# A graph network kernel: 28 blocks of plain-node rows made in round 3 instead of round 2

## The chip, the core and the metric

The program runs on one core of a Trainium2 chip. The metric is the device time of one execution in microseconds. Each engine (PE for matrix products, DVE and ACT for vector and scalar work, POOL, SP for issuing transfers) has its own instruction stream and waits for the others by semaphores.

## The reference, cut to what matters

Four graph layers follow each other, each added to its input and normalised. The second is a graph convolution that runs four rounds on 100,000 nodes of 64 numbers with 50,000 edges. Cut to it:

```python
def _L1_gnn_ref(x, edge_index, W, b, gamma, beta, num_rounds):
    loops = jnp.arange(n)
    src = jnp.concatenate([edge_index[0], loops])
    dst = jnp.concatenate([edge_index[1], loops])
    deg = segment_sum(ones, dst); dis = rsqrt(deg); norm = dis[src] * dis[dst]
    for _ in range(num_rounds):                     # 4 rounds
        h = x @ W
        agg = segment_sum(h[src] * norm[:, None], dst) + b
        x = layernorm(agg) * gamma + beta
    return x
x = _layernorm(x + _L1_gnn_ref(x, edge_index, ..., 4), axis=-1)
```

A node with no incoming edge has only its own loop: its row in a round is a product with W and a normalisation of its own row of the round before, with no gather. Here such rows are called plain. The kernel makes this plain form for every node, and the rows of nodes that are targets of edges are made in addition from gathered sums.

## The kernel before, in words

The convolution is done by `round_pass`, called as r1a and r1b (round 1 in two parts, which also make plain rows one round further), r2, r3 and r4, with a small `fix_pass` after a round that mends the rows in which a run of edges crosses partitions. Rounds don't overlap: `fix_pass` starts after SP and all engines are done with the round.

A pass goes over chunks of T = 14 columns of 128 edges each; there are 28 chunks (`CHUNKS`), two per step. For each chunk POOL issues 14 indirect gathers of 128 rows (line 2602), into four buffers of 7. DVE makes running sums along the edges, 7 columns at a time (`half`, line 2702, tile r_acc), adds the target's own row (`finish`, line 2735, tile r_gx), and the result is the input of the unit of targets.

A unit is a block of 128 x 14 rows, 128x896 numbers, that goes through: turned by PE (line 2851, tile r_ps_t), copied by ACT (2930, r_gt), multiplied by PE (2876, 2879 and 2882), squared by ACT (2936), summed over the features by DVE (2758), then root, reciprocal and a product with the result, tile r_y or, for targets, r_yt (2787 in round 2, 2789 in the others), and stored by SP. Each chunk has, besides its unit of targets, `nn` units of plain nodes and `ns` units of source rows (the nodes from which edges start, one row per edge), which SP loads (r_in). Units of one chunk come in the order plain, source, target. Before the change round 2 has nn = 2, ns = 1: four units per chunk. Round 3 has nn = 0, ns = 1: two.

In round 3 the source unit is also joined: its result for the whole layer is made at once. PE makes two products for it (dense1g into r_ps_v, gw into r_ps_g), DVE makes r_v (2774, 2776), adds the layer's input (r_r, 2779, loaded as r_x), sums again (2795) and writes r_y with one more number per row (2813, 2814). Round 3 also clears a table with SP's stores of r_blank. Round 2 keeps an extra copy of the product in SBUF by ACT (r_vs, 2939), so that the PSUM buffer is free early; round 3 doesn't.

The order on each engine is written out by `staged`: at each unit's slot an engine does one part for this unit, another for the unit some slots before. In slots behind the unit: PE turns 1 and multiplies 2 slots later, ACT squares 2 later, DVE sums and scales 3 later, the join ends 5 later, and SP stores 4 later (6 with a join). DVE's order within a slot is: sum of the product, sum of the join, running sums of this slot, end of the join, end of the unit. Every chunk's first half of running sums is done in the slot of the unit before the targets, its second half and r_gx in the targets' slot. Results go through two buffers of r_y (`y_free` waits until the one of two units ago is stored).

Of the kernel before, what the change touches and what calls it, by code (L numbers as in the profile page):

```python
# [9 lines left out]
D = 64  # L10
# [2236 lines left out]
def staged(eng, steps, units, most):  # L2247


    back = -(-most // units)  # L2250

    def run(body):
        def turn(i):
            for u in range(units):
                def ago(n):
                    at = i + (u - n) // units if (u - n) // units else i
                    out = isinstance(at, int) and not 0 <= at < steps
                    return () if out else ((at, (u - n) % units),)
                body(ago)
        for i in range(back + 1):  # L2260
            turn(i)
        if steps > back + 1:
            with eng.Fori(back + 1, steps) as i:
                turn(i)
        for i in range(steps, steps + back):
            turn(i)
    return run


CHUNKS = TILES // T  # L2270
# [136 lines left out]
                                             rest[:, 2, :].unsqueeze(1).to_broadcast([3, T, D])))  # L2407


def round_pass(nc, t, name, first_chunk, chunks, tkind, table, own, nkind, by_node, by_source, t_out, clear=None):  # L2410

# [1 line left out]
    nps = nn + ns  # L2415
    steps, units = chunks // 2, 2 * (nps + 1)
    first, tjoin, njoin = tkind == "first", tkind == "join", nkind == "join"
# [8 lines left out]
    with ExitStack() as ctx:  # L2426
        def sb(n, shape, dt=F32):
            return ctx.enter_context(nc.sbuf_tensor(f"{name}_{n}", shape, dt))
# [4 lines left out]
        def sems(n, count=2):  # L2433
            return [sem(f"{n}{u}") for u in range(count)]
# [19 lines left out]
        yt = sb("yt", [P, 2, T, D + 1 if tjoin else D])  # L2454
        y = sb("y", [P, 2, T, YW])
# [19 lines left out]
        in0_ok, y_stored = sems("in0_ok", units), sems("y_stored", units)  # L2475
# [16 lines left out]
        def is_t(u):  # L2492
            return u % (nps + 1) == nps

        def sub(u):
            return u // (nps + 1)

        def of_source(u):
            return nn <= u % (nps + 1) < nps

        def joined(u):
            return tjoin if is_t(u) else njoin

        def order(i, u):
            return i * (units // 2) + u // 2
# [7 lines left out]
        def after(eng, stage, i, u):  # L2513

            if valid(i):
                eng.wait_ge(stage[u % 2], order(i, u) + 1)
# [13 lines left out]
        def n_back(i, u, n):  # L2530

            for _ in range(n):
                i, u = back_to(i, u, 1, lambda w: not is_t(w))
            return i, u
# [2 lines left out]
            return bass.ds((first_chunk + i * 2 + s) * T, T)  # L2537

        def n_chunk(i, u):
            return (i * 2 + sub(u)) * nn + u % (nps + 1)  # L2540

        def s_columns(i, u):
            return bass.ds(((i * 2 + sub(u)) * ns + u % (nps + 1) - nn) * T, T)
# [1 line left out]
        def n_index(u):  # L2545
            return sub(u) * nps + u % (nps + 1)

        def slot(u):
            return n_index(u) % 2

        def j_slot(u):
            return u % 2 if tjoin else n_index(u) % 2

        def n_slot(u):
            return n_index(u) % IN
# [1 line left out]
        def nodes(tab, i, u):  # L2557
            features = X1 if tab is t.nodes1 else slice(0, D)
            return tab[0:NP, :].rearrange("(p j) w -> p j w", p=P)[:, bass.ds(n_chunk(i, u) * T, T), features]

        def nodes_of(tab, n):
            return tab[0:NP, :].rearrange("(p j) w -> p j w", p=P)[:, bass.ds(n * (J // CHUNKS), J // CHUNKS), :]

        def sources(tab, i, u, width):
            base = 2 * NP if tab is t.own1 else NP if tab is t.x2 else SOURCES
            features = X1 if tab is t.own1 else slice(0, width)
            return tab[base:base + EP, :].rearrange("(p j) w -> p j w", p=P)[:, s_columns(i, u), features]
# [9 lines left out]

        def tiles(flat):
            return flat.rearrange("p (t d) -> p t d", t=T)

        @block.gpsimd
        def _(pool):
# [41 lines left out]
        @block.sync  # L2624
        def _(sp):
            if clear is not None:
                sp.wait_ge(blank_made, 1)

            @staged(sp, steps, units, DEEP)
            def _(ago):  # L2630
                for i, u in ago(0):
                    s = sub(u)
                    if of_source(u) and clear is not None:
                        sp.dma_start(nodes_of(clear, i * 2 + s), blank[:]).then_inc(blanked, 16)
                    if not is_t(u):
                        after(sp, turned, *n_back(i, u, IN))
                        sp.sem_inc(sp_passed, 1)
                        given = sources(s_in, i, u, D) if of_source(u) else nodes(n_in, i, u)
                        sp.dma_start(in0[:, n_slot(u)], given).then_inc(in0_ok[u], 16)
                    elif not first:  # L2640
                        wait(sp, g_ready[s], i)
                        sp.sem_inc(sp_passed, 1)
                        sp.dma_start(mine[:, s], edges(own, i, s, D, NP)).then_inc(own_ok[s], 16)
                for i, u in ago(TURN):
                    s = sub(u)
                    if is_t(u):
                        sp.wait_ge(g_ready[s], i + 1)
                        sp.sem_inc(sp_passed, 1)
                        sp.dma_start(edges(t.g_rows, i, s, D), gx[:, s]).then_inc(g_stored[s], 16)
                        if first:  # L2650
                            sp.wait_ge(own_used[s], i + 1)
                            sp.wait_ge(own_kept[s], i + 1)
                            sp.sem_inc(sp_passed, 1)
                            sp.dma_start(edges(t.own_t, i, s, OWN), keep[:, s]).then_inc(own_stored[s], 16)
                for i, u in ago(PROD):
                    if joined(u):
                        after_join(sp, r_ready, *back_to(i, u, 2, joined))
                        sp.sem_inc(sp_passed, 1)
                        source = (edges(t.own_t, i, sub(u), OWN)[:, :, X1] if is_t(u) else
                                  sources(t.own1, i, u, D) if of_source(u) else nodes(t.nodes1, i, u))  # L2660
                        sp.dma_start(x1[:, j_slot(u)], source).then_inc(x1_ok[u], 16)
                for i, u in ago(DEEP):
                    s = sub(u)
                    if is_t(u) and not tjoin:
                        sp.wait_ge(y_ready[u], i + 1)
                        sp.sem_inc(sp_passed, 1)
                        sp.dma_start(edges(t_out, i, s, D, NP), yt[:, s]).then_inc(y_stored[u], 16)
                    elif not is_t(u):
                        sp.wait_ge(y_ready[u], i + 1)
                        sp.sem_inc(sp_passed, 1)  # L2670
                        made = sources(s_out, i, u, YW) if of_source(u) else nodes(n_out, i, u)
                        sp.dma_start(made, y[:, slot(u)]).then_inc(y_stored[u], 16)
            for u in range(units):
                if not (is_t(u) and tjoin):
                    sp.wait_ge(y_stored[u], steps * 16)
            if clear is not None:
                sp.wait_ge(blanked, CHUNKS * 16)
            for s in range(2):
                sp.wait_ge(g_stored[s], steps * 16)
                if first:  # L2680
                    sp.wait_ge(own_stored[s], steps * 16)

        @block.vector
        def _(dve):
# [52 lines left out]
            def y_free(i, u):  # L2737
# [4 lines left out]
                else:  # L2742
                    pi, pu = back_to(i, u, 2, lambda w: not is_t(w))
                    if valid(pi):
                        dve.wait_ge(y_stored[pu], (pi + 1) * 16)

            def result(i, u):
                return yt[:, sub(u)] if is_t(u) else y[:, slot(u)]

            if clear is not None:  # L2750
                nc.vector.memset(blank[:], 0.0).then_inc(blank_made, 1)
# [798 lines left out]
def gcn_rounds(nc, t):  # L3550
    recycle(nc)
    target_rows(nc, t)
    s1, s2, s3 = t.state[1:]
    round_pass(nc, t, "r1a", 0, CHUNKS // 2, "first", t.own1, t.own1, "step", (4, t.nodes1, s1), (2, t.own1, s1), s1)
    recycle(nc)
    round_pass(nc, t, "r1b", CHUNKS // 2, CHUNKS // 2, "first", t.own1, t.own1, "step", (4, s1, s2), (2, s1, s2), s1)
    recycle(nc)
    fix_pass(nc, t, "fix1", "first", s1)
    recycle(nc)
    round_pass(nc, t, "r2", 0, CHUNKS, "mid", s1, s1, "step", (2, s2, s3), (1, s2, s3), s2)  # L3560
    recycle(nc)
    fix_pass(nc, t, "fix2", "mid", s2)
    recycle(nc)
    round_pass(nc, t, "r3", 0, CHUNKS, "mid", s2, s2, "join", (0, None, None), (1, s3, t.x2), s3, clear=t.x2)
    recycle(nc)
    fix_pass(nc, t, "fix3", "mid", s3)
    recycle(nc)
    round_pass(nc, t, "r4", 0, CHUNKS, "join", s3, s3, "join", (2, s3, t.x2_plain), (0, None, None), t.x2)
    recycle(nc)
    fix_pass(nc, t, "fix4", "join", t.x2)  # L3570
# [91 lines left out]
```

## Time and profile before

| | us |
|---|---|
| median of 3 runs | 10783.97 (10775.03 to 10790.59) |
| the profiled execution | 10765.98 |
| its span | 10764.2 |
| busy PE, DVE, ACT, POOL | 5684.9, 6764.3, 2874.5, 7275.2 |

No engine is busy for more than 68% of the span: the kernel is a row of stages, each with its own limit, so a change in one stage is read from that stage. Round 2 lies between 5909 and 6558 us, round 3 between 6570 and 7113 us of the span. In the profile the tiles of both are named r_..., without the number of the round, so a stretch of time tells them apart.

### The profile page before, as it was taken

What the parts mean: (1) busy time and instruction counts of PE and PEld (TensorE: products, weight loads), DVE (VectorE), ACT (ScalarE), POOL (GpSimd) and SP (SyncE); (2) the same over time, 40 slices, a digit from 0 to 9 for tenths busy, and PEclk for the clock granted to TensorE, in tenths of its full rate; (3) what the DMA queues carried; (4) which work ended last, traced back from release to release, by engine and by line L of the source; (5) the groups of instructions that cost most, each with busy time, mean ns of one, the idle gap of its engine ahead of it and who ended that gap; (6) DMA issues with size and microseconds to landing.
All of it is one profiled execution on the core that took longest, in us unless ns stands there. A gap on an engine that the chain in (4) does not pass through costs nothing. (4 is left out here: it accounts for less than half of the span.)

```text
span 10764.2 us, 113652 instructions
## 1 busy us (share of the span) xinstructions
PE 5684.9 (53%) x26903; PEld 4008.1 (37%) x26903; DVE 6764.3 (63%) x14006; ACT 2874.5 (27%) x5217; POOL 7275.2 (68%) x7087
## 2 busy tenths in 40 slices
PE   3756999300000002877777776766764569622255
PEld 1453323000000001765555564555553447522234
DVE  8954333495878787987676666877775766411127
ACT  0042222001222223443333543222221322100045
POOL 3855777487777777767676765767777767677720
PEclk9978999655555555877777776777665655555578
DMA  0064333153545454437766665654445989511158
GB/s 14 4 235 121 73 71 73 20 196 107 166 145 168 145 165 133 128 118 210 203 211 198 204 204 178 231 165 139 133 132 167 314 219 125 86 46 46 46 197 242
DMA packets 1454719, 1555.31 MB, mean 144 GB/s; under 512 B 1037505, under 2 KB 1158687, under 8 KB 1454490
## 3 DMA queue, kind: packets, MB, share of 16 engines
q1 hardware_dynamic: 1191816, 1284.78, 37.6%
q0 software_dynamic: 252160, 248.38, 12.6%
q10 hardware_dynamic: 10514, 19.71, 0.5%
q8 instruction: 69, 1.13, 0.0%
q14 instruction: 160, 1.31, 0.0%
HBM read 883.57 MB, written 800.52 MB: 156 GB/s over the span
## 5 line engine op out<-in xcount | busy, mean ns | idle before, releaser
L2602 POOL DMA_INDIRECT r_got<-state,comb_src x1176 | 1187.9, 1010 | 431.0 <-issue 344.3
L312 POOL DMA_INDIRECT payload_or_bias_rows<-payload,place x784 | 938.6, 1197 | 484.5 <-issue 254.6
L1797 PE MATMUL hop_ps_into<-hop_out,span_s 128*128 128x256 f32 x8 | 4.9, 714 | 2054.1 <-DVE hop_out L1620 2054.1
L1446 POOL DMA_INDIRECT hop_got<-edges_b,next_col x784 | 829.7, 1058 | 261.4 <-issue 237.6
L1446 POOL DMA_INDIRECT hop_got<-edges_a,next_col x784 | 784.6, 1001 | 259.4 <-issue 238.2
L1797 PEld LDWEIGHTS hop_ps_into<-hop_out,span_s 128*128 128x128 f32 x8 | 2.0, 310 | 2056.4 <-DVE hop_out L1620 2056.4
L1684 ACT COPY hop_got<-hop_zeros 128x1792 f32<-128x1792 f32 x224 | 378.1, 1688 | 1116.0 <-DVE hop_ps_msg L1571 1106.5
L1620 DVE SCALAR_TENSOR_TENSOR hop_out<-hop_out,hop_runs_now,hop_ps_msg 128x256 f32<-128x256 f32 x1176 | 565.6, 481 | 50.9
L2882 PE MATMUL r_ps_v<-dense1g,r_gt 128*128 128x128 f32 x3136 | 588.9, 361 | 0.0
L2882 PEld LDWEIGHTS r_ps_v<-dense1g,r_gt 128*128 128x128 f32 x3136 | 534.8, 264 | 134.2 <-issue 134.2
L2702 DVE SCALAR_TENSOR_TENSOR r_acc<-r_acc,r_runs_now,r_got 128x64 f32<-128x64 f32 x1173 | 334.7, 285 | 278.4 <-DMA r_got<-state,comb_src 235.3
L1571 DVE TENSOR_TENSOR hop_ps_msg<-hop_ps_side,hop_got 128x1792 f32<-128x1792 f32 x168 | 341.5, 2033 | 250.2 <-DMA hop_got<-edges_a,next_col 166.8
L2610 POOL DMA_INDIRECT x<-r_yt,put_t x392 | 414.7, 1058 | 119.5 <-issue 119.5
L3137 POOL DMA_INDIRECT c_got<-x,row_t x392 | 410.5, 1047 | 122.3 <-issue 119.2
L1208 DVE SCALAR_TENSOR_TENSOR sc_leaky<-sc_raw 4x896 f32<-4x896 f32 x56 | 60.5, 1081 | 674.8 <-ACT sc_raw L1161 674.8
L1117 POOL DMA_INDIRECT sc_got<-own,t_col x392 | 392.3, 1001 | 129.8 <-issue 129.1
L3349 POOL DMA_INDIRECT c_got<-cheb_rows,next_col x392 | 379.0, 967 | 135.7 <-issue 119.2
L1458 POOL DMA_INDIRECT x_and_sums<-gin_out,put_s x392 | 389.4, 993 | 119.5 <-issue 119.5
L1117 POOL DMA_INDIRECT sc_got<-own,s_col x392 | 383.9, 979 | 121.1 <-issue 119.8
L1449 POOL DMA_INDIRECT gin_got<-x,row_t x392 | 374.6, 956 | 123.6 <-issue 119.2
L1769 PE MATMUL gin_ps_gt<-ident,gin_got 128*64 128x128 f32 x392 | 93.7, 417 | 646.9 <-DMA gin_got<-x,row_t 646.9
L1232 PE MATMUL sc_psz<-sc_xt,w_ht 64*128 64x512 f32 (+1 forms) x896 | 403.7, 580 | 6.4 <-DVE sc_sort_taken L360 6.4
(816 smaller groups left out, 17759.0 us busy)
## 6 DMA issues: line engine op xcount, KB each, us to landing
edges_a<-hop_out SPq DMA_DIRECT2D x112, 896.0 KB
edges_b<-hop_out SPq DMA_DIRECT2D x112, 896.0 KB, 4.3
r_in<-state SPq DMA_DIRECT2D x168, 448.0 KB, 4.5
hop_side<-x_dst SPq DMA_DIRECT2D x280, 224.0 KB
own<-plain_y SPq DMA_DIRECT2D x56, 952.0 KB
x_and_sums<-c_y SPq DMA_DIRECT2D x56, 896.0 KB, 5.1
bn_in<-x_and_sums SPq DMA_DIRECT2D x56, 896.0 KB
r1a_in<-own SPq DMA_DIRECT2D x84, 448.0 KB, 4.6
```

Source lines behind the costliest of these rows:

```text
L312: nc.gpsimd.indirect_dma_start(out=t.raw[:, n, :], out_offset=None, in_=t.pay[k], in_offset=bass.IndirectOffsetOnAxis(t.place[:, k, n:n + ...
L1117: pool.indirect_dma_start(out=got[:, u, c, cols], out_offset=None, in_=flat, in_offset=bass.IndirectOffsetOnAxis(by[:, at], 0)).then_inc(g ...
L1232: ins = nc.tensor.matmul(psz[:, z, b, 0:hi - lo], t.w_ht[half, m * P:(m + 1) * P], xt[half, u, lo:hi], start=True, stop=True)
L1446: pool.indirect_dma_start(out=got[:, u, c, :], out_offset=None, in_=table, in_offset=at, bounds_check=EP - 1, oob_is_err=False).then_inc(g ...
L1458: pool.indirect_dma_start(out=target, out_offset=bass.IndirectOffsetOnAxis(put[:, n * CT + c:n * CT + c + 1], 0), in_=out[:, u % 2, c, :], ...
L1620: nc.vector.scalar_tensor_tensor(acc[:, u % 2, c, 0:M], before, runs_now[:, u % 2, c:c + 1], terms[:, c, :], ALU.mult, ALU.add).then_inc(l ...
L1684: nc.scalar.copy(got[:, u], zeros[:]).then_inc(zeroed[u], 1)
L2602: pool.indirect_dma_start(out=got[:, n, c - b * CT, :], out_offset=None, in_=table, in_offset=bass.IndirectOffsetOnAxis(idx[:, at + c:at + ...
L2610: pool.indirect_dma_start(out=t_out, out_offset=bass.IndirectOffsetOnAxis(t.put_t[:, at + c:at + c + 1], 0), in_=yt[:, s, c, :], in_offset ...
L2882: ins = nc.tensor.matmul(out[:, n * P:(n + 1) * P], gt[:, k, n * P:(n + 1) * P], wts[:], start=False, stop=True, skip_group_check=True)
L3137: pool.indirect_dma_start(out=got[:, n % RING, c, :], out_offset=None, in_=t.x2, in_offset=bass.IndirectOffsetOnAxis(t.row_t[:, n * CT + c ...
L3349: pool.indirect_dma_start(out=got[:, u, c, :], out_offset=None, in_=t.cheb_rows, in_offset=bass.IndirectOffsetOnAxis(t.next_col[:, n * CT ...
```

## The change

Round 2 makes one plain unit per chunk (nn = 1), the 28 blocks 0 to 27. The other 28 blocks, 28 to 55, are made in round 3, by the new argument `first_rows`, also one per chunk and also from s2 into s3. Round 3 thus has units of three kinds per chunk: plain (not joined), source (joined), target (not joined). `joined` now says so, the join's buffers go by the chunk's place in the step, and the plain result is written to the first 64 of the 65 numbers per row that r_y has in this round.

```diff
-def round_pass(nc, t, name, first_chunk, chunks, tkind, table, own, nkind, by_node, by_source, t_out, clear=None):
+def round_pass(nc, t, name, first_chunk, chunks, tkind, table, own, nkind, by_node, by_source, t_out, clear=None, first_rows=0):
...
         def joined(u):
-            return tjoin if is_t(u) else njoin
+            return tjoin if is_t(u) else njoin and (of_source(u) or not ns)
...
         def n_chunk(i, u):
-            return (i * 2 + sub(u)) * nn + u % (nps + 1)
+            return first_rows + (i * 2 + sub(u)) * nn + u % (nps + 1)
...
         def j_slot(u):
-            return u % 2 if tjoin else n_index(u) % 2
+            return u % 2 if tjoin else sub(u) if ns else n_index(u) % 2
...
+        def result(i, u):
+            return yt[:, sub(u)] if is_t(u) else y[:, slot(u)] if of_source(u) else y[:, slot(u), :, 0:D]
...
-                        sp.dma_start(made, y[:, slot(u)]).then_inc(y_stored[u], 16)
+                        sp.dma_start(made, result(i, u)).then_inc(y_stored[u], 16)
...
-    round_pass(nc, t, "r2", 0, CHUNKS, "mid", s1, s1, "step", (2, s2, s3), (1, s2, s3), s2)
+    round_pass(nc, t, "r2", 0, CHUNKS, "mid", s1, s1, "step", (1, s2, s3), (1, s2, s3), s2)
...
-    round_pass(nc, t, "r3", 0, CHUNKS, "mid", s2, s2, "join", (0, None, None), (1, s3, t.x2), s3, clear=t.x2)
+    round_pass(nc, t, "r3", 0, CHUNKS, "mid", s2, s2, "join", (1, s2, s3), (1, s3, t.x2), s3, clear=t.x2,
+               first_rows=CHUNKS)
```

The line numbers of `round_pass` from 2577 to 2750 move by up to three (2702 becomes 2705, 2735 becomes 2738). DVE in round 2, from the sum of the targets' product (the one with att_edges behind it) to r_gx of the next chunk, before:

```order
L2758 TENSOR_REDUCE r_stat<-r_sq 128x14
L2761 SCALAR_TENSOR_TENSOR r_stat<-r_stat,att_edges 128x14
L2702 SCALAR_TENSOR_TENSOR r_acc<-r_acc,r_runs_now,r_got 128x64 x7
L2769 RECIPROCAL r_stat<-r_stat 128x14
L2782 TENSOR_TENSOR r_stat<-r_stat,att_edges 128x14
L2787 SCALAR_TENSOR_TENSOR r_yt<-r_vs,r_stat 128x896
L2758 TENSOR_REDUCE r_stat<-r_sq 128x14
L2764 TENSOR_SCALAR r_stat<-r_stat 128x14
L2702 SCALAR_TENSOR_TENSOR r_acc<-r_acc,r_runs_now,r_got 128x64 x7
L2735 SCALAR_TENSOR_TENSOR r_gx<-r_acc,r_own 128x896
```

The same place after the change, with the source unit's sum and the first half of running sums ahead of it:

```order
L2758 TENSOR_REDUCE r_stat<-r_sq 128x14
L2764 TENSOR_SCALAR r_stat<-r_stat 128x14
L2705 SCALAR_TENSOR_TENSOR r_acc<-r_acc,r_runs_now,r_got 128x64 x7
L2769 RECIPROCAL r_stat<-r_stat 128x14
L2787 SCALAR_TENSOR_TENSOR r_y<-r_vs,r_stat 128x896
L2758 TENSOR_REDUCE r_stat<-r_sq 128x14
L2761 SCALAR_TENSOR_TENSOR r_stat<-r_stat,att_edges 128x14
L2705 SCALAR_TENSOR_TENSOR r_acc<-r_acc,r_runs_now,r_got 128x64 x7
L2738 SCALAR_TENSOR_TENSOR r_gx<-r_acc,r_own 128x896
```

The targets' sum now stands directly before the second half; the first half has moved ahead of it, and yt behind r_gx.

DVE in round 3, from the sum of the source unit's product to r_gx, before (r_rstat belongs to the join of the source unit one chunk earlier):

```order
L2758 TENSOR_REDUCE r_stat<-r_sq 128x14
L2764 TENSOR_SCALAR r_stat<-r_stat 128x14
L2795 TENSOR_REDUCE r_rstat<-r_rsq 128x14
L2797 TENSOR_SCALAR r_rstat<-r_rstat 128x14
L2702 SCALAR_TENSOR_TENSOR r_acc<-r_acc,r_runs_now,r_got 128x64 x7
L2735 SCALAR_TENSOR_TENSOR r_gx<-r_acc,r_own 128x896
```

and after the change:

```order
L2758 TENSOR_REDUCE r_stat<-r_sq 128x14
L2764 TENSOR_SCALAR r_stat<-r_stat 128x14
L2705 SCALAR_TENSOR_TENSOR r_acc<-r_acc,r_runs_now,r_got 128x64 x7
L2769 RECIPROCAL r_stat<-r_stat 128x14
L2774 TENSOR_TENSOR r_v<-r_ps_g,r_stat 128x896
L2776 SCALAR_TENSOR_TENSOR r_v<-r_v,beta_c 128x896
L2779 SCALAR_TENSOR_TENSOR r_r<-r_v,r_x 128x896
L2758 TENSOR_REDUCE r_stat<-r_sq 128x14
L2761 SCALAR_TENSOR_TENSOR r_stat<-r_stat,att_edges 128x14
L2705 SCALAR_TENSOR_TENSOR r_acc<-r_acc,r_runs_now,r_got 128x64 x7
L2738 SCALAR_TENSOR_TENSOR r_gx<-r_acc,r_own 128x896
```

The first half of running sums, r_v and r_r and the targets' sum now lie between the source unit's sum and r_gx; the join's own sum (r_rstat) has moved behind r_gx.

PE in round 3 after the change, from the turn of r_gx on: the two products of the source unit, then the plain unit's turn and the targets' product as before, then the source unit's turn and one product more, the plain one:

```order
L2851 MATMUL r_ps_t<-ident,r_in 128x128 x7
L2876 MATMUL r_ps_g<-bt,r_rows_now 128x512
L2876 MATMUL r_ps_g<-bt,r_rows_now 128x384
L2882 MATMUL r_ps_g<-dense1g,r_gt 128x128 x7
L2851 MATMUL r_ps_t<-ident,r_in 128x128 x7
L2879 MATMUL r_ps_g<-brow,ones 128x512
L2879 MATMUL r_ps_g<-brow,ones 128x384
L2882 MATMUL r_ps_g<-dense1g,r_gt 128x128 x7
```

Its last four rows are new in this round.

## Rows read from the trace of the kernel before

**Rows 1.** Busy time by stretch: round 2 and round 3; columns in the first line.
```profile
core 0: us, PE busy (x) PEld busy (x) DVE busy (x) ACT busy (x) POOL busy (x), PEclk, DMA share, GB/s
5909.00:6558.00 649.00, 498.33 (x2634) 385.21 (x2634) 426.80 (x897) 309.89 (x505) 411.04 (x392) 0.77 0.62 198
6570.00:7113.00 543.00, 377.40 (x1792) 284.07 (x1792) 417.48 (x871) 148.94 (x280) 384.61 (x392) 0.72 0.64 214
```

**Rows 2.** POOL's waits in round 2 (first two), then in round 3.
```profile
engine line waited for: us in total, times, longest us
POOL r_got L2602 <- issue: 112.5, 368, 0.5
POOL r_got L2602 <- DVE r_acc L2702: 70.0, 23, 5.9
...
POOL r_got L2602 <- DVE r_acc L2702: 4.9, 16, 0.3
```

**Rows 3.** Gathers of line 2602 in round 2, then in round 3.
```profile
engine op xcount: duration ns min/median/max, first and last start us, forms
L2602 POOL DMA_INDIRECT r_got<-state,comb_src x392: 942/947/1759, 5909.4 to 6502.0; - x196
...
L2602 POOL DMA_INDIRECT r_got<-state,comb_src x392: 943/947/1782, 6570.0 to 7072.9; - x196
```

**Rows 4.** Line 2735 (r_gx) in round 2, then round 3; columns as in Rows 3.
```profile
L2735 DVE SCALAR_TENSOR_TENSOR r_gx<-r_acc,r_own x28: 1091/1092/1093, 5930.5 to 6536.1; 128x896 f32<-128x896 f32 x28
...
L2735 DVE SCALAR_TENSOR_TENSOR r_gx<-r_acc,r_own x28: 1091/1092/1093, 6591.1 to 7082.2; 128x896 f32<-128x896 f32 x28
```

**Rows 5.** Timeline of DVE, one chunk of round 2.
```profile
start us, us, engine line op out<-in xcount [idle before <-releaser]
6218.52 1.09 DVE L2735 SCALAR_TENSOR_TENSOR r_gx<-r_acc,r_own 128x896 f32<-128x896 f32 x1
...
6233.93 1.09 DVE L2758 TENSOR_REDUCE r_stat<-r_sq 128x14 f32<-128x896 f32 x1 [4.97 <-ACT r_sq L2936]
...
6235.67 2.21 DVE L2702 SCALAR_TENSOR_TENSOR r_acc<-r_acc,r_runs_now,r_got 128x64 f32<-128x64 f32 x7 [0.30 <-issue]
...
6240.79 2.21 DVE L2702 SCALAR_TENSOR_TENSOR r_acc<-r_acc,r_runs_now,r_got 128x64 f32<-128x64 f32 x7
```

**Rows 6.** Timeline of DVE in round 3.
```profile
6812.70 1.09 DVE L2735 SCALAR_TENSOR_TENSOR r_gx<-r_acc,r_own 128x896 f32<-128x896 f32 x1
...
6829.40 1.09 DVE L2735 SCALAR_TENSOR_TENSOR r_gx<-r_acc,r_own 128x896 f32<-128x896 f32 x1
...
6831.85 0.23 DVE L2769 RECIPROCAL r_stat<-r_stat 128x14 f32<-128x14 f32 x1
...
6835.38 1.08 DVE L2758 TENSOR_REDUCE r_stat<-r_sq 128x14 f32<-128x896 f32 x1
...
6836.97 2.21 DVE L2702 SCALAR_TENSOR_TENSOR r_acc<-r_acc,r_runs_now,r_got 128x64 f32<-128x64 f32 x7 [0.18 <-issue]
...
6839.78 1.09 DVE L2789 TENSOR_TENSOR r_yt<-r_ps_g,r_stat 128x896 f32<-128x896 f32 x1
6842.67 1.09 DVE L2758 TENSOR_REDUCE r_stat<-r_sq 128x14 f32<-128x896 f32 x1 [1.79 <-ACT r_sq L2936]
...
6846.73 2.21 DVE L2702 SCALAR_TENSOR_TENSOR r_acc<-r_acc,r_runs_now,r_got 128x64 f32<-128x64 f32 x7 [1.44 <-DMA r_got<-state,comb_src]
6848.97 1.09 DVE L2735 SCALAR_TENSOR_TENSOR r_gx<-r_acc,r_own 128x896 f32<-128x896 f32 x1
```

**Rows 7.** Timeline of PE in round 3.
```profile
6821.55 1.83 PE L2882 MATMUL r_ps_g<-gw,r_gt 128*128 128x128 f32 x14
...
6833.36 0.90 PE L2879 MATMUL r_ps_v<-brow,ones 3*128 3x512 bf16 x2 [1.74 <-DVE r_v L2774]
...
6838.32 3.36 PE L2882 MATMUL r_ps_g<-gw,r_gt 128*128 128x128 f32 x14
```

**Rows 8.** Groups by line and form: the source unit's two products, round 3.
```profile
line engine op names shapes xcount | busy us, mean ns | idle before us <-releasers
L2882 PE MATMUL r_ps_v<-dense1g,r_gt 128*128 128x128 f32 x392 | 93.8, 432 | 0.0
L2882 PE MATMUL r_ps_g<-gw,r_gt 128*128 128x128 f32 x392 | 74.1, 363 | 0.0
```

**Rows 9.** Timeline of PE in round 2, after a gap.
```profile
6490.96 1.75 PE L2851 MATMUL r_ps_t<-ident,r_gx 128*128 128x128 f32 x7 [4.89 <-DVE r_gx L2735]
...
6497.75 1.77 PE L2876 MATMUL r_ps_v<-bt,r_rows_now 28*128 28x512 f32 x4
```

**Rows 10.** DMA queue q1 in round 2, then in round 3.
```profile
## 3 DMA queue, kind: packets, MB, share of 16 engines
q1 hardware_dynamic: 36288, 115.62, 52.4%
...
q1 hardware_dynamic: 74816, 103.38, 54.6%
```

More of the change, by code:

```diff
@@ L2745, in y_free @@
                         dve.wait_ge(y_stored[pu], (pi + 1) * 16)
-            def result(i, u):
-                return yt[:, sub(u)] if is_t(u) else y[:, slot(u)]
             if clear is not None:
```

## The prediction

> **What bounds the two rounds now.** I read the busy time by stretch first. Round 2 lasts 649 us (5909 to 6558) and round 3 lasts 543 us (6570 to 7113), and no engine is full in either: the fullest are PE in round 2 (498 us) and DVE in round 3 (417 us) [rows 1]. The page's chain of waits ends in the last stage of the kernel and doesn't reach the rounds, so I go by the rounds' own waits. POOL's row of waits parts them: it waited 70.0 us for the running sums (r_acc) in round 2 and 4.9 us in round 3 [rows 2]. Round 3 is therefore paced by its 392 gathers, which begin between 6570.0 and 7072.9; with the last one's 0.95 us that is 503.8 us, 1.285 us each. In round 2 the same 392 take from 5909.4 to 6503.0, 593.6 us [rows 3]. Each round passes through 28 chunks, and the first and last r_gx (one per chunk) give the period of a chunk: (6536.1-5930.5)/27 = 22.43 us in round 2 and (7082.2-6591.1)/27 = 18.19 us in round 3 [rows 4]. What lies before the first r_gx is 21.1 us in both; what lies behind the last is 22 us and 31 us [rows 1, 4]. I leave these ends as they are; after the last r_gx only the unit of sources and the unit of targets remain, in both versions.
>
> **Round 2, three units per chunk instead of four.** The timelines of DVE and PE show one closed loop. r_gx ends at 6219.61; PE turns it, multiplies the source unit, turns a plain one and multiplies the target unit; ACT squares; DVE's sum starts at 6233.93 after a wait of 4.97 us. DVE then does the first half of the next chunk's running sums, the target rows' yt, the plain unit's sum, and the second half at 6240.79 with r_gx behind it at about 6243.0 [rows 5]. That is 24.5 us in this chunk, 22.43 on average. In the changed order nothing stands between the target unit's variance and the second half: the stretch from 6235.67 to 6240.79, 5.1 us, leaves the loop (its work is done earlier, in the 4.97 us that DVE waited). 22.43-5.1 = 17.3 us, below the pace of the gathers, so POOL becomes the bound. Its pace is 14 gathers: 18.0 us at round 3's 1.285 us, 18.9 us if round 2's mean busy time of 411.04/392 = 1.05 us plus the 0.30 us between two (112.5/368) stays [rows 1, 2]. I take 18.4, between them, since DVE's work per chunk in round 2 comes nearer to round 3's, where a gather was busy 384.61/392 = 0.98 us. Round 2: 27 x (22.43-18.4) = 109 us less; bounds 27 x (22.43-18.9) = 95 and 27 x (22.43-18.0) = 120 us. The removed 28 units' 28 loads and 28 stores free the queue of SP; nothing waited for it here.
>
> **Round 3, three units per chunk instead of two.** It gains 28 times a turn, a product, ACT's copy and square, and on DVE a sum (1.09 us), two small operations (0.17 and 0.23) and y (1.09), about 2.7 us with gaps. DVE's 417.48 us over 28 chunks are 14.9 us each [rows 1], to 17.6: that alone would still lie under 18.19. But the place matters. Before, the loop is: r_gx ends at 6830.49, PE waits for r_v until 6833.36, does the two products of the source unit until 6841.68 (8.3 us), ACT squares, DVE's sum starts at 6842.67; then two sums with their small operations (2.4 us, worked out from their 1.09 us and gaps), the half (2.2) and r_gx (1.1) [rows 6, 7]. This took 19.57 us, 18.1 without its wait of 1.44 us for a gather. A chunk whose second product ran at the quicker rate (1.83 us for 14 matmuls instead of 3.36) took 16.70 [rows 6, 7], or 16.4 without its 0.30. Both are about at the gathers' 18 us, which is why POOL hardly waits.
> In the changed order DVE has four things between the source unit's sum and the next r_gx: first half (2.2 us), the join's r_v and r_r with its reciprocal (3.53 us, 6831.85 to 6835.38), the target unit's sum (1.5 us, 6835.38 to about 6836.9) and the second half [rows 6]. The stretch before the second half grows from 2.4 to 1.2+2.2+3.5+1.4 = 8.3 us, by 5.9. On the other side PE no longer waits for r_v after r_gx (2.9 us) but for yt, some 1.8 us after it (in the old place it ends at 6840.87, 1.7 us after the half that ends at 6839.18, [rows 6]), 1.0 us less with the step between. Net 4.9 us more: 16.4 to 21.3 us, and 18.1 to 23.0 us. POOL, at 18, no longer sets the pace. Which of the two it is hangs on PE's clock. Round 3's first product took 3.35 us always (93.8/28) and its second 74.1/28 = 2.65 us, so 54% of them slow [rows 8]; that share gives 22.2 us. After the change PE has one gap of 4 to 5 us per chunk, as in round 2, where after the gap before 6490.96 the target unit's product was already quick 7 us later (1.77 us at 6497.75) [rows 9]; quick again in eight of ten chunks would give 21.6. I take 21.9: 27 x (21.9-18.19) = 100 us more, bounds 27 x (21.3-18.19) = 84 and 27 x (23.0-18.19) = 130 us. Its two ends stay at 21 and 32 us.
> Smaller edits: the plain unit's y is written with rows of 65 numbers (taken at the same 1.09 us on DVE). SP's queue gets a load and a store more per chunk. The store stands behind SP's wait for r_gx, and after it come the block of zeros and the next source load, both needed half a chunk later. The page shows 214 GB/s in round 3 [rows 1]; 28 x 2 x 0.459 MB more make it 142 MB in 640 us, 222 GB/s, so transfers are not the bound.
>
> **The sum.** -109+100 = -9 us. The profiled execution took 10765.98 us (its span 10764.2), so 10757 us in its terms; the median of the runs lies 18 us above it, so 10775 us. I write 10776.
>
> **A store in small pieces.** The plain unit's rows lie 65 apart in SBUF, so its store goes in pieces of 256 bytes. The nearest rows are loads: r_x is read as 14 pieces of 256 bytes per partition and is in round 3's q1, which needed 54.6% of 543 us for 103.38 MB, 2.87 us per MB; round 2's q1, without such pieces, needed 52.4% of 649 us for 115.62 MB, 2.94 us per MB [rows 10]. By these rows a small piece costs nothing, though they say it of reads. The Trainium skill, in "DMA: Bandwidth & Descriptors" (Specifications), says that below 512 B the engine does a read-modify-write; if this holds for these stores each would take longer than any row here shows.
>
> **Rivals.** (A) Faster: PE stays quick and the join's loop closes in under 21 us. For it: DVE's own work is 17.6 us plus gaps, about 18.6, so the floor is 27 x 0.4 = 11 us more. Against it: the first product took 3.35 us on average [rows 8], so hardly one was quick. With a quick first product in four of ten chunks (1.5 us each) the period is 20.7 us, round 3 takes 68 us more, and the sum is -41: 10743 us. (B) Slower: the plain unit's y buffer. DVE writes y about 6.3 us after r_gx (yt, the plain unit's sum, the join's sum and y), and must wait until the y of one chunk ago is stored; SP issues that store only after its wait for the same r_gx, behind g_rows and r_x. Three transfers of 448 KB at the 214 GB/s of [rows 1] take 6.4 us and land about 8 us after r_gx. The next sum on DVE is free to start at 9 to 11 us, so this costs from about 9.5 us of landing onward. Small pieces that take twice as long would land it at 10 to 11, y would end at 12, and 1 to 2 us per chunk come on top: round 3 +130 to +150, sum +30 to +45, about 10820 us. (C) Nothing moves but the place, because both rounds miss by halves: round 2 keeps 18.9 and round 3 takes 22.5 (+116): +21, 10805 us. (D) Round 3 hides the whole unit behind its gathers: -100 or so, 10680 us; only if the order on DVE didn't matter.
>
> **How the numbers follow.** The forecast with its neighbourhood (10755 to 10800) has 0.46, A 0.24, D 0.05, C and B together 0.25 (B 0.13). A difference under 0.2%, 22 us, can't be told from none. A and D are faster, 0.29; the forecast is the same, 0.46; B and C slower, 0.25. The range takes in most of A and of B: 10733 to 10822 us.
>
> **What would show it.** Round 2 should last about 540 us, with POOL waiting under 15 us for r_acc and DVE's longest wait for r_sq under 5; if POOL still waits 40 us, the loop was longer than 17.3. Round 3 should last about 643 us, its r_gx 21.3 to 23 us apart, POOL waiting over 70 us for r_acc, and in each chunk r_gx, yt, first product 1.8 us later, sum, half, r_v, r_r, sum, half. A wait of DVE before the plain y for a store shows B. Wrong would be a round 3 under 610 us or over 665, or a change in any stage outside the two rounds.

## The result and the profile after

The changed kernel takes 10929.0 us (median of 4 runs, 10922.52 to 10933.58) against 10781.95 us for the kernel before in the same comparison: ratio 1.0136, 95% interval 1.0118 to 1.0153. It is 147 us slower; forecast was no change.

First the busy time by stretch, for round 2 and round 3 of the changed kernel (to hold against [rows 1]):

```profile
core 0: us, PE busy (x) PEld busy (x) DVE busy (x) ACT busy (x) POOL busy (x), PEclk, DMA share, GB/s
5908.00:6474.00 566.00, 392.87 (x1990) 301.78 (x1990) 356.57 (x785) 236.75 (x392) 419.36 (x392) 0.74 0.59 182
6486.00:7244.00 758.00, 527.59 (x2437) 396.39 (x2438) 486.81 (x983) 202.07 (x364) 410.05 (x392) 0.70 0.60 187
```

Round 2 went from 649 to 566 us, round 3 from 543 to 758 us. From each round's first gather to the `fix_g` behind it the lengths are 648.8 and 543.8 us before, 566.2 and 758.3 after: -82.6 and +214.5, together +132. That leaves 15 us of the 147. The two profiled executions lie 164 us apart, and there the rest lies behind the rounds: from the last `fix_g` (behind round 4) to the end 2580 us in the profiled execution of before and 2616 in this one. In the ten experiments this stretch, in which nothing was changed, takes 2586 to 2604 us. So it moves from one execution to the next; why it does is not shown. The prediction had named a change outside the two rounds as a sign of being wrong.

POOL's waits in round 2, then in round 3 (line, who was waited for, us in total, times, longest), against [rows 2]:

```profile
engine line waited for: us in total, times, longest us
POOL r_got L2605 <- issue: 119.2, 391, 0.3
```

```profile
POOL r_got L2605 <- DVE r_acc L2705: 162.1, 23, 8.5
```

In round 2 POOL no longer waits for DVE at all: the gathers are the bound, as forecast, but each is busy for 419.36/392 = 1.07 us. In round 3 POOL waits 162 us. What DVE waited for there, longest first:

```profile
engine line waited for: us in total, times, longest us
DVE r_y L2789 <- DMA x<-r_y: 183.0, 27, 8.3
DVE r_stat L2758 <- ACT r_sq L2936: 23.6, 22, 8.2
```

The first row is the answer. DVE waits 183 us, 27 times, 6.8 us each, before it makes the plain unit's y; and the releaser is not the plain unit's own store (state<-r_y) but x<-r_y, the store of the join's result. One chunk in round 3 on DVE, then on SP (start, duration, line, names, idle time ahead and its releaser):

```profile
6845.20 1.09 DVE L2738 SCALAR_TENSOR_TENSOR r_gx<-r_acc,r_own 128x896 f32<-128x896 f32 x1
...
6846.78 1.09 DVE L2789 TENSOR_TENSOR r_yt<-r_ps_g,r_stat 128x896 f32<-128x896 f32 x1
...
6851.14 1.14 DVE L2814 SCALAR_TENSOR_TENSOR r_y<-r_r,r_rstat 128x896 f32<-128x896 f32 x1
6852.21 0.23 DVE L2769 RECIPROCAL r_stat<-r_stat 128x14 f32<-128x14 f32 x1
6858.46 1.09 DVE L2789 TENSOR_TENSOR r_y<-r_ps_g,r_stat 128x896 f32<-128x896 f32 x1 [6.02 <-DMA x<-r_y]
6859.47 1.08 DVE L2758 TENSOR_REDUCE r_stat<-r_sq 128x14 f32<-128x896 f32 x1
...
6865.56 1.09 DVE L2779 SCALAR_TENSOR_TENSOR r_r<-r_v,r_x 128x896 f32<-128x896 f32 x1
...
6870.93 1.09 DVE L2738 SCALAR_TENSOR_TENSOR r_gx<-r_acc,r_own 128x896 f32<-128x896 f32 x1
```

```profile
6846.56 0.33 SPq L2652 DMA_DIRECT2D g_rows<-r_gx  x1
6847.15 0.41 SPq L2664 DMA_DIRECT2D r_x<-own  x1
6847.83 0.75 SPq L2675 DMA_DIRECT2D state<-r_y  x1
6848.78 2.56 SPq L2637 DMA_DIRECT2D x<-r_blank  x1
6851.61 0.37 SPq L2642 DMA_DIRECT2D r_in<-state  x1
6852.53 0.62 SPq L2675 DMA_DIRECT2D x<-r_y  x1
```

DVE ends the join's y at 6852.28. SP issues its store at 6852.53, behind the transfers of r_gx, r_x, the plain y of the chunk before, the zeros and a load. It lands some 6 us later, and only then, at 6858.46, does DVE write the plain y, into a buffer that this store doesn't read. The cause is in `y_free`: it goes two units back and, where that is a unit of targets, two more (`back_to(i, u, 2, ...)`). With three units per chunk that leads from the plain unit to the source unit of the chunk before, which uses the other buffer; its result, in the join, is made in the very slot in which the plain y is due.

So `y_free` doesn't always wait for "the one of two units ago", as the description of the kernel has it. Before the change the two steps missed too: in round 3, with two units per chunk, they lead from a source unit to the source unit of one chunk ago, which uses the other buffer. That store had been issued early enough: in round 3 of before no wait of DVE for a store shows at all. The change made a wrong partner that was free into one that is dear.

### The profile page after: what moved, and what is told of

It is laid out like the page before. It is cut to its first block and busy times, and to the rows that moved or that the text cites. A ratio compares the mean times of both kernels' runs of the same rounds, so it can differ in the third digit from the quotient of the medians.

```text
span 10928.4 us, 113680 instructions
## 1 busy us (share of the span) xinstructions
PE 5737.5 (53%) x26903; PEld 4033.4 (37%) x26903; DVE 6759.8 (62%) x14006; ACT 2855.0 (26%) x5189; POOL 7290.1 (67%) x7087
## 5 line engine op out<-in xcount | busy, mean ns | idle before, releaser
L2605 POOL DMA_INDIRECT r_got<-state,comb_src x1176 | 1217.9, 1036 | 522.9 <-issue 351.0
L2882 PE MATMUL r_ps_v<-dense1g,r_gt 128*128 128x128 f32 x2744 | 508.5, 358 | 0.0
L2882 PEld LDWEIGHTS r_ps_v<-dense1g,r_gt 128*128 128x128 f32 x2744 | 461.3, 261 | 114.4 <-issue 114.4
```

Of the source, the lines that this page charges most:

```text
L2605: pool.indirect_dma_start(out=got[:, n, c - b * CT, :], out_offset=None, in_=table, in_offset=bass.IndirectOffsetOnAxis(idx[:, at + c:at + ...
L2882: ins = nc.tensor.matmul(out[:, n * P:(n + 1) * P], gt[:, k, n * P:(n + 1) * P], wts[:], start=False, stop=True, skip_group_check=True)
```

## The experiments

All kernels were run beside the kernel before; a ratio is to it. Round lengths are from the first gather to the `fix_g` behind.

| kernel | median us, before us | ratio | round 2 | round 3 |
|---|---|---|---|---|
| before | | | 648.8 | 543.8 |
| changed | 10929.0, 10782.0 | 1.0136 (1.0118 to 1.0153) | 566.2 | 758.3 |
| right wait | 10779.2, 10761.3 | 1.0016 (1.0006 to 1.0026) | 570.7 | 633.2 |
| early store | 10836.6, 10761.3 | 1.0071 (1.0054 to 1.0088) | 566.0 | 696.1 |
| whole rows | 10863.3, 10761.3 | 1.0090 (1.0073 to 1.0107) | 573.3 | 731.0 |
| two loads | 10906.2, 10760.4 | 1.0135 (1.0118 to 1.0152) | 564.0 | 764.7 |
| round 3 alone | 10980.4, 10761.3 | 1.0199 (1.0182 to 1.0216) | 651.5 | 751.2 |
| right wait, early store | 10781.4, 10761.7 | 1.0016 (1.0006 to 1.0026) | 567.3 | 634.4 |
| right wait, tensor_tensor | 10774.3, 10761.7 | 1.0012 (1.0003 to 1.0022) | 567.0 | 634.9 |
| source first | 10725.4, 10761.7 | 0.9965 (0.9951 to 0.9979) | 568.6 | 585.1 |
| source first, early store | 10725.0, 10761.7 | 0.9965 (0.9951 to 0.9980) | 566.2 | 581.4 |
| source first, no copy | 10690.2, 10760.4 | 0.9933 (0.9916 to 0.9949) | 526.7 | 585.0 |

**Right wait.**

```diff
-                    pi, pu = back_to(i, u, 2, lambda w: not is_t(w))
+                    pi, pu = n_back(i, u, 2) if njoin and not tjoin else back_to(i, u, 2, lambda w: not is_t(w))
```

> One edit: in round 3, y_free waits for the store of the unit that last used the same buffer of r_y (two non-target units ago), instead of what the step of two slots finds, which from the plain unit is the source unit of the chunk before. Theory W (the wait is on the wrong store: DVE waits 183 us in round 3 for the join's store that it has itself only just released): that wait goes, the chunk's period in round 3 falls from 26.2 to about 22 us, round 3 from 758 to about 645 us, the time to 10800 to 10830 us. Rival S (the plain unit's own store in pieces of 256 bytes is late, as rival B of the prediction had it): the wait stays under another name, 10890 to 10930 us.

Round 3 falls by 125 us, the ratio from 1.0136 to 1.0016. Theory W holds: its 10800 to 10830 us were reckoned on a before of 10782, so 18 to 48 us above before, and this kernel is 18 above. (The edit also gives the join's y the store of its own buffer to wait for; in the changed kernel it waited for the plain unit's of the chunk before.) The wait before the plain y that is left is of the kind of rival S, for its own store, but a fifth of it. DVE's longest waits in round 3 of this kernel:

```profile
engine line waited for: us in total, times, longest us
DVE r_stat L2758 <- ACT r_sq L2936: 41.8, 26, 6.5
DVE r_y L2789 <- DMA state<-r_y: 39.5, 27, 3.3
```

The two rows add up to 81.3 us; the two of the changed kernel (183.0 and 23.6) to 206.6. The difference, 125 us, is what round 3 gained.

The median period of a chunk is 21.2 us, the mean (7099.0-6514.6)/27 = 21.64 us: the loop as the prediction had it, 21.9.

**Early store.**

```diff
-                    elif not is_t(u):
+                    elif not is_t(u) and not soon(u):
...
+                for i, u in ago(NORM + 1):
+                    if soon(u):
+                        sp.wait_ge(y_ready[u], i + 1)
+                        sp.sem_inc(sp_passed, 1)
+                        sp.dma_start(nodes(n_out, i, u), result(i, u)).then_inc(y_stored[u], 16)
```

> One edit: in round 3 SP stores the plain unit's result four slots behind the unit instead of six, so it is issued half a chunk earlier; the wait of DVE is left as it is. Theory W: DVE doesn't wait for this store, so the time stays at 10929 within 25 us. Rival S: the store lands long before the buffer is wanted, the period falls to about 22 us and the time to 10800 to 10830 us.

Neither: 0.65% faster than the changed kernel, where W said unchanged and S said 100 us or more. DVE's row still names the join's store, with less time:

```profile
DVE r_y L2797 <- DMA x<-r_y: 132.0, 27, 6.5
```

In the changed kernel a plain y is stored only a chunk after it is made, just ahead of the next join's store (6847.83 and 6852.53 above). Here it is stored as soon as it is made, some 6 us behind the join's store of that slot, so it is no longer under way when the next join's store is issued:

```profile
6826.66 0.33 SPq L2655 DMA_DIRECT2D g_rows<-r_gx  x1
...
6832.47 0.33 SPq L2678 DMA_DIRECT2D x<-r_y  x1
6838.38 0.38 SPq L2683 DMA_DIRECT2D state<-r_y  x1
```

The median from issue to landing of x<-r_y falls from 6.5 to 4.6 us. So which store is waited for was W's, and S's store was part of how long it took.

**Whole rows, and its control with two loads.** The first gives the plain y a tile of its own with rows of 64, and two instead of four buffers for loads to make room; the second only the latter.

```diff
+            yp = sb("yp", [P, 1, T, D])
...
-    IN = {1: 2, 2: 4, 3: 3, 6: 4}[nps]
+    IN = 2 if njoin and not tjoin else {1: 2, 2: 4, 3: 3, 6: 4}[nps]
...
+            return yt[:, sub(u)] if is_t(u) else y[:, slot(u)] if of_source(u) else yp[:, 0, :, 0:D] if plain_own else y[:, slot(u), :, 0:D]
```

> In round 3 the plain unit's result has a buffer of its own with rows of 64 numbers, so its store goes in pieces of 3584 bytes per partition instead of 256 bytes; to make room the loads of units have two buffers instead of four. The waits are left as they are. Theory W: only what the queue of transfers gains is seen, 0 to 30 us faster than 10929. Rival S: 60 to 110 us faster. If small pieces are costly, the DMA queue q1 also shows a smaller share than its 52.7% of 758 us.

> The changed kernel with two instead of four buffers for the loads of units in round 3, and nothing else: the part of the kernel with whole rows that only makes room. If it costs nothing, the ratio to before is 1.0136 as in the changed kernel (within 0.002), round 3 lasts 750 to 760 us, and the gain of the kernel with whole rows (1.0136 to 1.009) is the rows' alone. If it is 1.010 or less, the gain was the buffers'.

The control has the ratio of the changed kernel (its round 3, at 764.7 us, is 5 above the 750 to 760 expected), so the 0.45% are the rows'. These 49 us are more than W said (30) and less than S (60); round 3 itself is 27 us shorter than in the changed kernel and 34 shorter than in the control. DMA queue q1 in round 3 (packets, MB, share of 16 engines), of the changed kernel and of the one with whole rows:

```profile
q1 hardware_dynamic: 129472, 129.07, 52.7%
```

```profile
q1 hardware_dynamic: 82880, 129.07, 51.0%
```

52.7% of 758 us are 399.5 us, 51.0% of 731 us are 372.8 us, for the same bytes: 26.7 us over 28 stores, 0.95 us each. At the second kernel's 372.8/129.07 = 2.89 us per MB, a whole store takes 1.33 us of the sixteen engines and one in pieces 2.3 us, 1.7 times as long. The prediction had read from its rows on loads that a small piece costs nothing. That was a misreading: 2.87 and 2.94 us per MB are means over two different mixes. The trace's records of single packets part them. In round 3 of before, the 50176 packets of 256 bytes, all of r_x, took 19.9 ns each in the mean, 4.9 us of the sixteen engines per MB, and the 14336 packets of 3584 bytes 149.4 ns, 2.6 us per MB. So loads in these pieces took nearly twice as much per byte too; round 2's packets of 3584 bytes were slower (167.6 ns), which hid it. The sentence of the Trainium skill ("DMA: Bandwidth & Descriptors", Specifications: below 512 B a read-modify-write) points the right way. That it is a read-modify-write which costs the time, no run here shows.

**Round 3 alone.**

```diff
-    round_pass(nc, t, "r2", 0, CHUNKS, "mid", s1, s1, "step", (1, s2, s3), (1, s2, s3), s2)
+    round_pass(nc, t, "r2", 0, CHUNKS, "mid", s1, s1, "step", (2, s2, s3), (1, s2, s3), s2)
```

> Round 3 makes its 28 plain units as in the change, but round 2 still makes all 56, so 28 blocks are made twice with the same values. If the cost lies in round 3 alone and the rounds don't act on each other, the time is that of before plus round 3's 214 us: 10782 + 214 = 10996 us, within 20. If part of round 3's length came from what round 2 leaves behind, it is below 10970.

219 us above its own before (214 were expected): the rounds add up. Round 3 costs 207 us here whatever round 2 does.

**Right wait and early store.** The edits are the two above.

> The right wait (DVE waits for the store of the unit that last used this buffer) and the early store of the plain unit (four slots behind it instead of six) together, in round 3. With the right wait alone DVE still waited 39.5 us for the plain unit's own store, 1.5 us per chunk. If that wait is in the loop, it goes and the period falls from 21.6 to about 20.5 us, the time by 25 to 30 us against the right wait alone (1.0016 of before), so 0.998 to 1.000 of before. If the wait only fills time in which DVE would wait for the square of the source unit's product, the period stays above 21.3 and the ratio at 1.001 to 1.002.

The same as the right wait alone, 1.0016. DVE's wait for the plain store goes (39.5 us), and the wait for ACT's squares (r_sq) rises from 41.8 to 80.4 us: the wait for the store only filled time that the loop leaves free.

```profile
DVE r_stat L2766 <- ACT r_sq L2944: 80.4, 28, 8.2
```

**Source first**, with the right wait, and the same with the early store.

```diff
-            return nn <= u % (nps + 1) < nps
+            return u % (nps + 1) < ns if ahead else nn <= u % (nps + 1) < nps
...
+    ahead = njoin and ns > 0
```

> The right wait, and in round 3 the units of a chunk in the order source, plain, target instead of plain, source, target. The theory of the loop (r_gx, the source unit's two products, its square and sum, then the first half, the join and the target's sum before the next r_gx) says that the two products and the join then leave the loop, which holds the plain unit's single product, the target's product and sum: 14 to 19 us. What is left is DVE's own work, about 18.6 us per chunk, and the gathers' pace. Period 19 to 20.3 us, round 3 575 to 600 us, time 0.995 to 0.998 of before. Rival: the period of 21.6 is set by the sum of work on PE or DVE and not by the order; then it stays at 21 to 22 and the ratio at 1.001 to 1.003.

> As the kernel with the source unit first, with the early store of the plain unit besides. If the plain unit's store is still waited for there, 10 to 25 us faster than that kernel; else the same within 8 us. At best 0.993 of before.

Round 3 falls from 633 to 585 us, the period from 21.64 to (7029.3-6494.3)/27 = 19.8 us, with the same instructions in another order. Busy time of PE, DVE, ACT and POOL in round 3 with the source first:

```profile
core 0: us, PE busy (x) PEld busy (x) DVE busy (x) ACT busy (x) POOL busy (x), PEclk, DMA share, GB/s
6473.00:7058.00 585.00, 446.49 (x2438) 342.93 (x2438) 486.58 (x983) 203.20 (x364) 399.85 (x392) 0.81 0.79 243
```

DVE's 486.58 us are those of the changed kernel (486.81), so no work went; it waits less. PE's wait for r_gx, with the right wait alone and then with the source unit first:

```profile
PE r_ps_t L2851 <- DVE r_gx L2738: 129.3, 28, 7.6
```

```profile
PE r_ps_t L2852 <- DVE r_gx L2739: 42.7, 28, 3.6
```

PE's granted clock is also a little higher, 0.81 of full speed against 0.78 with the right wait alone; how much of the 48 us is the clock's and how much the order's is not separated. 0.9965 is faster than before. The early store adds nothing that can be told.

**Right wait and tensor_tensor in round 2.**

```diff
-                        nc.vector.scalar_tensor_tensor(result(i, u), vs[:, k], 1.0, per_node(stat[:, k, 3, :]), ALU.mult, ALU.mult).then_inc(y_ready[u], 1)
+                        nc.vector.tensor_tensor(result(i, u), vs[:, k], per_node(stat[:, k, 3, :]), ALU.mult).then_inc(y_ready[u], 1)
```

> The right wait in round 3, and in round 2 DVE's product that makes r_y and r_yt from the copy in SBUF is a tensor_tensor instead of a scalar_tensor_tensor with a factor of 1. In round 2 of the changed kernel POOL never waits for DVE, and 70 of 80 of these products have a slow gather beside them (48 of 53 r_y and 22 of 26 r_yt). Theory: a gather that is issued during a scalar_tensor_tensor of 896 numbers with both inputs in SBUF isn't through before it ends, and this is what makes a gather 1.07 instead of 0.95 us. If tensor_tensor doesn't do this, the gathers of round 2 fall to about 0.99 us, round 2 from 571 to about 540 us and the time by 30 us against the right wait alone (0.999 of before). If it does it alike, or if the cause is something else that goes on at those moments (an issue of SP), round 2 stays at 566 to 573 us.

Round 2 stays at 567 us, and 49 of 56 r_y and 25 of 28 r_yt still have a slow gather (over 1.05 us) beside them; in the whole of the changed kernel's round 2 it was 49 of 56 and 22 of 28. This left two readings: both instructions do it, or neither.

**Source first, no copy.**

```diff
-    keeps = not joins and not first
+    keeps = False
```

> As the kernel with the right wait and the source unit first, and in round 2 ACT's copy of the product (r_vs) is left out: DVE makes r_y and r_yt from PSUM, as in round 3. Theory: what slows the gathers of round 2 is a DVE product of 896 numbers with both inputs in SBUF; three of four per chunk then have one input in PSUM, the gathers fall from 1.07 to 0.97 to 1.0 us, round 2 from 568 to 525 to 545 us, and the ratio from 0.9965 to 0.993 to 0.995. Rival: PE must now wait for DVE's r_yt before the next product, the loop of round 2 gets longer than the gathers' 18 us, and round 2 stays at 565 or more; or the gathers are slowed by SP's issues, then they stay at 1.07 us and round 2 at 568.

Round 2 falls to 526.7 us. The busy times in it, with the columns named, and an extract of POOL and of DVE from round 2 of the changed kernel:

```profile
core 0: us, PE busy (x) PEld busy (x) DVE busy (x) ACT busy (x) POOL busy (x), PEclk, DMA share, GB/s
5903.00:6430.00 527.00, 392.54 (x1989) 302.17 (x1990) 358.10 (x786) 175.55 (x310) 383.24 (x392) 0.76 0.61 195
```

```profile
6203.50 0.94 POOL L2605 DMA_INDIRECT r_got<-state,comb_src  x1 [0.30 <-issue]
6204.75 1.30 POOL L2605 DMA_INDIRECT r_got<-state,comb_src  x1 [0.30 <-issue]
...
6208.84 0.95 POOL L2605 DMA_INDIRECT r_got<-state,comb_src  x1 [0.30 <-issue]
...
6211.33 1.84 POOL L2605 DMA_INDIRECT r_got<-state,comb_src  x1 [0.30 <-issue]
6213.48 0.94 POOL L2605 DMA_INDIRECT r_got<-state,comb_src  x1 [0.30 <-issue]
```

```profile
6204.14 1.09 DVE L2787 SCALAR_TENSOR_TENSOR r_y<-r_vs,r_stat 128x896 f32<-128x896 f32 x1
...
6208.87 2.21 DVE L2705 SCALAR_TENSOR_TENSOR r_acc<-r_acc,r_runs_now,r_got 128x64 f32<-128x64 f32 x7
...
6211.26 1.09 DVE L2787 SCALAR_TENSOR_TENSOR r_y<-r_vs,r_stat 128x896 f32<-128x896 f32 x1
6212.57 1.08 DVE L2758 TENSOR_REDUCE r_stat<-r_sq 128x14 f32<-128x896 f32 x1 [0.21 <-ACT r_sq L2936]
```

With y made from PSUM a gather is busy 383.24/392 = 0.98 us instead of 1.07. In the extract the gathers begun at 6204.75 and 6211.33 last 1.30 and 1.84 us, and each of them begins during a product r_y<-r_vs; both end 0.82 us after that product does (6205.23 and 6212.35). The ones beside r_acc last 0.94. Of the 392 gathers of this kernel's round 2, 20 are slow, all 20 begun during r_gx, which has both inputs in SBUF still; in the changed kernel's round 2 it was 86 of 392. This answers both rivals that the edit alone leaves, ACT's copy (which went with it) and SP's issues: gathers beside r_gx are slow as before though the copy is gone, and those begun during the products from PSUM take at most 0.95 us. PE's new waits (r_y 8.5, r_yt 7.7 us) are small.

## Why the prediction was wrong, by its steps

- **Round 2, the loop.** Right: POOL waits 0 us for DVE, where 70.0 was before.
- **Round 2, the gain.** Forecast 109 us with a period of 18.4, bounds 95 to 120; measured 82.6, with 14 x (1.07+0.30) = 19.2 us per chunk, outside the bounds. The mis-sized term is the gathers' pace, 1.07+0.30 us. I took it that with fewer products in DVE the gathers would get quicker, and put the worst case at round 2's old mean of 1.05 us. The products with both inputs in SBUF did get fewer (140, now 112), but the gathers begun during one and slowed by it got more: 70 of 392 before, 86 after. What counts is how much of the product is left when a gather begins, and that moved with the order; why it fell out this way is not shown. The last experiment shows what slows them: with y made from PSUM, round 2 is 526.7 us.
- **Round 3, the loop.** Right in kind and size once the wait is mended: forecast 21.9 us per chunk and +100 us; the kernel with the right wait has 21.64 and 633.2-543.8 = +89 us. With the source unit first the period is 19.8 us (+41) and PE waits 42.7 us for r_gx instead of 129.3; that fits the two products and the join leaving the loop.
- **Round 3, the buffer of y.** This step failed, and it is most of the error. The prediction had DVE wait "until the y of one chunk ago is stored", the plain unit's own store, which SP issues just after r_gx; it put the price at 0 unless small pieces were slow, and gave it 0.13 as rival B at 10820 us. The wait is for the store of the join's y, whose data DVE finishes 0.2 us before it begins to wait. DVE does its work in order, so nothing of it goes on during the landing: 6.8 us per chunk, 183 us by DVE's row, and 125 us of round 3's length by the run that takes it away; the rest comes back as other waits. Order and code both showed it before the run: `back_to` with a step of 2 in a chunk of three units.
- **Small pieces.** Rival B's other half is real but second: 1.7 times the engines' time per store, 0.45% of the time through the queue ahead of the join's store. With the right wait DVE does wait for this store as B said, 39.5/27 = 1.5 us per chunk (B: 1 to 2), but not on top: the run with both edits takes the wait away and is no faster. That small pieces cost nothing by the rows on loads was read wrongly (see the whole rows).
- **Transfers not the bound.** Right: 187 GB/s in round 3, and with the source unit first the same 142 MB went at 243 GB/s, more than the 222 that the prediction allowed for.
- The sum: -83+214 = +132 us by the rounds where the forecast was -9. Of these 141 us, 115 are round 3's and 26 round 2's. With the right wait the rounds give -78+89 = +11 and the time 18 us above before: without the wait on the wrong store the two errors left are 26 us in round 2 and 11 in round 3, the other way.

Not tried: round 2's part alone, since the blocks that it no longer makes are then missing; its share rests on the trace and on the run with round 3 alone.

## What to carry to other kernels

When a loop gets another kind of unit, work out for each wait on a buffer which instruction it now names, by index and not by its comment or aim. A wait on the wrong partner can leave the results right and show in the time alone; here nothing waits for the plain unit's own store before its buffer is written again, and by the code only its being issued ahead of the store that is waited for guards it. A transfer just issued that is waited for cost its whole landing here, in each turn. And where two stages trade work, compare the loops they are in: with the right wait, the same instructions in two orders of units gave 1.0016 and 0.9965.

## What the runs showed of the hardware

A gather issued by POOL during a DVE operation on 128x896 numbers with both inputs in SBUF took up to 1.85 us instead of 0.95: it ended about 0.82 us after the operation did. tensor_tensor and scalar_tensor_tensor did it alike, and with one input in PSUM nearly all such gathers were gone (20 of 392 slow instead of 86). I had not expected this for tensor_tensor, nor that leaving out a copy on ACT would be worth 42 us of a round through POOL. Stores in pieces of 256 bytes took 1.7 times the DMA engines' time of the same store in pieces of 3584, and loads in pieces of 256 bytes 4.9 us per MB where pieces of 3584 took 2.6.
